# RK4 stage of a conditioned four-layer kernel: linear values written into PSUM by VectorE instead of identity products on TensorE

## What is computed

```
def _derivative(q, p, drive, coupling, bias):
    i_couple = jnp.tanh(q) @ coupling.T
    dq = q - q ** 3 / 3.0 - p + drive + i_couple + bias
    dp = EPSILON * (q + ALPHA - BETA * p)
    return (dq, dp)

def _rk4_step(q, p, drive, coupling, bias):
    dq1, dp1 = _derivative(q, p, drive, coupling, bias)
    dq2, dp2 = _derivative(q + 0.5 * DT * dq1, p + 0.5 * DT * dp1, ...)
    dq3, dp3 = _derivative(q + 0.5 * DT * dq2, p + 0.5 * DT * dp2, ...)
    dq4, dp4 = _derivative(q + DT * dq3, p + DT * dp3, ...)
    q_next = clip(q + DT / 6.0 * (dq1 + 2 * dq2 + 2 * dq3 + dq4))
    p_next = clip(p + DT / 6.0 * (dp1 + 2 * dp2 + 2 * dp3 + dp4))
```

## Time and profile before

| what | us |
|---|---|
| three runs | 912.86, 912.0, 912.5 (median 912.5) |
| the profiled execution's own time | 913.69 |
| its span in the trace | 911.7 |
| RK4 stage, all 32 steps | from about 720 to 908 |
| PE busy | 895.2 |
| DVE busy | 605.3 |
| ACT busy | 411.8 |
| POOL busy | 276.8 |

### The profile page before, as it was taken

One profiled execution on the slowest core, in us unless ns is written; L12 is line 12 of the kernel. 1 busy time (PEld: TensorE's weight loads), 2 busy tenths in 40 slices (PEclk: granted clock), 3 DMA queues, 4 the chain that ended last, 5 costly groups with the idle time before them and its releaser, 6 DMA issues.

```text
span 911.7 us, 18478 instructions
## 1 busy us (share of the span) xinstructions
PE 895.2 (98%) x7182; PEld 766.0 (84%) x7182; DVE 605.3 (66%) x1697; ACT 411.8 (45%) x1144; POOL 276.8 (30%) x359
## 2 busy tenths in 40 slices
PE   7999999999999999999999999999999999999998
PEld 5788888888888888888887778899986699999998
DVE  5544555654565544746477875677777788888887
ACT  2233322333223432224346654555545676666665
POOL 2654500011000300014312424333213455554443
PEclk9999999999999999999999999999999999999999
DMA  7222100000000000110014000000000000000000
GB/s 270 75 77 79 39 1 1 2 1 1 2 1 2 1 1 1 47 47 2 1 38 159 0 1 1 1 1 2 1 1 1 1 2 24 1 25 1 25 1 24
DMA packets 5703, 22.00 MB, mean 24 GB/s; under 512 B 880, under 2 KB 1264, under 8 KB 5232
## 3 DMA queue, kind: packets, MB, share of 16 engines
q1 hardware_dynamic: 5616, 20.82, 6.6%
HBM read 18.72 MB, written 2.10 MB: 23 GB/s over the span
## 4 chain that ended last, share of the span: by engine, by line
PE 90%; DVE 7%; ACT 2%; issue 1%; DVEq 0%
PE ps L366 43%; PE ps L774 8%; PE ps L778 7%; PE ps L457 6%; PE ps L635 6%; PE ps L773 5%; PE ps L625 3%; PE ps L637 3%; PE ps L446 2%; DVE g_lo L1273 1%; PE ps L642 1%; PE ps L378 1%; DVE m_lo L1267 1%; DVE frs L1245 1%; PE ps L373 1%
## 5 line engine op out<-in xcount | busy, mean ns | idle before, releaser
L1190 DVE TENSOR_SCALAR qk<-ps,vec 128x512 f32<-128x512 f32 x64 | 48.0, 749 | 99.0 <-PE ps L366 99.0
L366 PE MATMUL ps<-x_hi,W_hi 128*128 128x512 f32 x256 | 102.1, 399 | 3.2 <-DVE x_lo L1313 2.8
L856 ACT ACTIVATE qk<-ps,vec 128x512 f32<-128x512 f32 x64 | 44.2, 690 | 124.9 <-PE ps L366 124.9
L366 PE MATMUL ps<-x_hi,W_lo 128*128 128x512 f32 x256 | 99.8, 390 | 0.0
L366 PE MATMUL ps<-x_lo,W_hi 128*128 128x512 f32 x256 | 99.8, 390 | 0.0
L774 PE MATMUL ps<-rk_th,cpc 128*128 128x128 f32 x516 | 99.0, 294 | 0.1
L1201 DVE SCALAR_TENSOR_TENSOR o_lo<-ps,vec,o_hi 128x512 fp32r<-128x512 f32 x64 | 47.1, 744 | 72.7 <-ACT o_hi L872 69.1
L872 ACT ACTIVATE o_hi<-ps,vec 128x512 fp32r<-128x512 f32 x64 | 44.1, 688 | 111.9 <-PE ps L457 111.9
L774 PEld LDWEIGHTS ps<-rk_th,cpc 128*128 128x128 f32 x516 | 72.7, 191 | 9.3 <-ACT rk_th L1136 6.2
L635 PE MATMUL ps<-ht,hh 128*128 128x128 f32 x512 | 77.0, 283 | 1.0 <-DVE ht L1525 0.9
L773 PE MATMUL ps<-rk_th,cpc 128*128 128x64 f32 x508 | 77.8, 255 | 0.0
(11 more groups left out here) (281 smaller groups left out, 2134.1 us busy)
## 6 DMA issues: line engine op xcount, KB each, us to landing
stage<-qkv_w SPq DMA_DIRECT2D x6, 768.0 KB, 4.5
stage<-out_w SPq DMA_DIRECT2D x4, 512.0 KB, 3.9
f_raw<-ffn_w SPq DMA_DIRECT2D x2, 1024.0 KB, 4.8
xorig<-xT SPq DMA_DIRECT2D x1, 2048.0 KB, 8.2
x_all<-xT SPq DMA_DIRECT2D x1, 1536.0 KB, 15.2
out<-xtb SPq DMA_DIRECT2D x3, 512.0 KB, 3.1
ada_sb<-ada_w SPq DMA_DIRECT2D x1, 1024.0 KB, 9.6
BD<-qkv_w SPq DMA_DIRECT2D x1, 768.0 KB, 6.1
```

The source lines that it names most:

```text
L366: r = pe.matmul(out_, lhsT, rhs, start=first and i == 0, stop=last and i == n - 1)
L856: act.activation(qk[:, 0, h % 2, :], ps[:, PJ[0], :], ACT.Identity, bias=col("qkv_b", HU * u + h)).then_inc(act_evac, 1)
L1190: dve.tensor_scalar(qk[:, 1, h % 2, :], ps[:, PJ[1], :], col("qkv_b", HEADS + HU * u + h), None, ALU.add).then_inc(dve_evac, 1)
```

## The change

In evaluations 1 to 4 of every step DVE writes `E1`, `Z2`, `Z3`, `Z4` straight to the PSUM columns 0 to 63 of the two banks of that evaluation (`seed`), and the identity products go. The coupling products then all run with `start=False` and add to what stands there. Two exceptions are in the first step: evaluation 1 keeps `first_evaluation`, and evaluation 2 keeps `linear(2, "Z2")`. Columns 64 to 127 of these banks, which the `twice` products also write, are never read. After the coupling products of every evaluation but the very first stand five passes of zeros (`keep_warm(WARM_RK)`). `skip_group_check=True` is an argument for the builder and no instruction.

```
-WARM_GRU, WARM_START = 10, 12
+WARM_GRU, WARM_START, WARM_RK = 10, 12, 5
...
             def chunks_in_turn(t, k):
...
                 coupled(k, 1, 1, False, True).then_inc(rk_pe, 1)
+                keep_warm(WARM_RK)
...
             def chunks_together(t, k):
...
                 coupled(k, 1, 1, False, True).then_inc(rk_pe, 1)
+                keep_warm(WARM_RK)
...
                     pe.wait_ge(rk_dve, RK_START + at(t - 1, RK_DVE, "E1"))
-                    linear(1, "E1")
                     chunks_together(t, 1)
...
                 pe.wait_ge(rk_dve, RK_START + at(t, RK_DVE, "Z2"))
-                linear(2, "Z2")
                 if t == 0:
+                    linear(2, "Z2")
                     keep_warm(WARM_START)
                 chunks_in_turn(t, 2)
                 pe.wait_ge(rk_dve, RK_START + at(t, RK_DVE, "Z3"))
-                linear(3, "Z3")
                 chunks_together(t, 3)
                 pe.wait_ge(rk_dve, RK_START + at(t, RK_DVE, "Z4"))
-                linear(4, "Z4")
                 chunks_in_turn(t, 4)
...
+            def seed(k):
+                lo = RK_BANK[k % 2][0]
+                return ps[:, lo:lo + KC, 0:B]
...
-                inc(STT(r_["Z2"], r_["q"], 1 - A_ * C_, r_["U2"], M, Ad))
+                inc(STT(seed(2) if t else r_["Z2"], r_["q"], 1 - A_ * C_, r_["U2"], M, Ad))
...
-                inc(STT(r_["Z3"], r_["q2"], -A_ * C_, r_["t3"], M, Ad))
+                inc(STT(seed(3), r_["q2"], -A_ * C_, r_["t3"], M, Ad))
...
-                inc(STT(r_["Z4"], r_["q3"], 2 * (1 - A_ * C_), r_["b4"], M, Ad))
+                inc(STT(seed(4), r_["q3"], 2 * (1 - A_ * C_), r_["b4"], M, Ad))
...
-                inc(dve.tensor_tensor(r_["E1"], r_[f"D{(t + 1) % 3}"], r_["P"], Su))
+                inc(dve.tensor_tensor(seed(1), r_[f"D{(t + 1) % 3}"], r_["P"], Su))
```

More of the change, by code:

```diff
@@ L772, in coupled @@
                 if last:
-                    return pe.matmul(ps[:, RK_BANK[k % 2][c], 0:B], w, th, start=first, stop=last)
-                return pe.matmul(ps[:, RK_BANK[k % 2][c], 0:2 * B], w, twice(th), start=first, stop=last)
+                    return pe.matmul(ps[:, RK_BANK[k % 2][c], 0:B], w, th, start=first, stop=last, skip_group_check=True)
+                return pe.matmul(ps[:, RK_BANK[k % 2][c], 0:2 * B], w, twice(th), start=first, stop=last, skip_group_check=True)
             def linear(k, z):
                 for c in range(KC):
-                    pe.matmul(ps[:, RK_BANK[k % 2][c], 0:2 * B], ident[:, :], twice(rk[z][:, c, :]), start=True, stop=False)
+                    pe.matmul(ps[:, RK_BANK[k % 2][c], 0:2 * B], ident[:, :], twice(rk[z][:, c, :]), start=True, stop=False, skip_group_check=True)
             def tanh_done(t, k, half):
@@ L808, in first_evaluation @@
                 for c in range(KC):
-                    pe.matmul(ps[:, RK_BANK[1][c], 0:B], ident[:, :], rk["E1"][:, c, :], start=False, stop=True).then_inc(rk_pe, 1)
+                    pe.matmul(ps[:, RK_BANK[1][c], 0:B], ident[:, :], rk["E1"][:, c, :], start=False, stop=True, skip_group_check=True).then_inc(rk_pe, 1)
             for t in range(T):
```

## The result

The change makes the kernel slower: 917.76 us (median of 5 runs, 916.1 to 918.1) against 912.86 for the kernel before in the same comparison. The ratio is 1.0038, 95% interval 1.0023 to 1.0053; the two medians alone would give 1.0054, since the executions before spread from 912.0 to 916.0, so the ratio (3.5 us) is the figure to go by.

A forecast was written before the change was run, and what follows sets the result against it. The prediction took the ring of DVE, ACT and PE latencies as the bound, PE's throughput just under it. Only the moved wait cost: 63 x 0.065 = 4.1 us on 912.5 gave 916.6 us, range 912.2 to 919.5.

The forecast's parts named there:

- The ring: One RK4 step: DVE, ACT and PE latencies from result to reader close at 5.86 us, without the identity products of L778.
- The identity products: PE, evaluations 1 to 4: removing 1.8 us of PE work a step was forecast to gain zero.
- DVE's writes to PSUM: E1, Z2, Z3, Z4 on DVE: taken as zero, with 0.01 us each way for Z2 and Z4, 0.6 us in all.
- the stretches of 1.32 and 1.12: DVE's own chain from qraw to q2 and from q3 to q4, in us, forecast to stay unchanged.
- Zeros: Five passes on PE after the coupling products: about 0.33 us with the entry, forecast to cost nothing in time.
- the 0.04 that the prediction allowed in evaluation 3: Extra us the entry to the zeros could cost on PE before they delayed evaluation 3's coupling load.
- The clock: Rival: PE rests more and its granted clock falls to half; 919 us for one or two falls, chance 0.05.
- The wait that moves: PE's tanh wait, written second, becomes a separate instruction: 0.065 us in the ring in evaluations 2 and 4, 4.1 us in all.
- The 63 places: Evaluations 2 and 4 of every step except evaluation 2 of the first, each paying 0.065 us: 4.1 us.
- The prediction's 0.08 for the same thing on DVE: DVE's next instruction starts 0.11 us after release by a separate wait against 0.03 with its own: difference 0.08.
- PE as the bound: Rival: q2 and q4 hang on PE, so removing identity products gains 7.1 us; 909.5 us with the waits, chance 0.08.
- The cheap wait of 0.02: Rival: PE's separate tanh wait costs only 0.02 us a place, 1.3 us in all, 913.8 us; chance 0.14.

The follow-up runs named there:

- e1: The changed kernel with PE's two waits written the other way round, tanh first and linear value second: 912.14 us, ratio 0.9993, step 5.859 us.
- e2: The changed kernel without PE's waits for the linear value from step 1 on: 913.31 us, ratio 1.0000, step 5.862 us.
- e4: The changed kernel without the passes of zeros (WARM_RK = 0): 916.32 us, ratio 1.0035, step 5.984 us.
- e3: The kernel before with a redundant wait for the linear value ahead of the tanh wait in evaluations 2 and 4: 916.39 us, ratio 1.0037.
- e6: e2 with DVE's two waits ahead of the first half of q2 swapped, its own w first: 912.38 us, ratio 0.9981, step 5.796 us.
- e5: The kernel before with DVE's two waits ahead of the first half of q2 swapped, its own w first: 912.16 us, ratio 0.9984.
- e8: e6 with DVE's U2 moved ahead of the second half of qraw, where DVE waits for PE: 914.91 us, ratio 1.0022, step 5.943 us.
- e7: e5 with DVE's U2 moved ahead of the second half of qraw, identity products kept: 918.1 us, ratio 1.0050, step 6.021 us.
- e11: e8 with POOL's U3 waiting for the moved U2, no identity products: 916.34 us, ratio 1.0025, step 5.946 us.
- e12: e7 with POOL's U3 waiting for the moved U2, identity products kept: 919.1 us, ratio 1.0050, step 6.021 us.

## Why the prediction was right

Forecast 916.6 us in a range from 912.2 to 919.5; measured 917.76. Point by point:

- **The ring, and what is not in it.** Right. It closed before and closes after, and only the pieces named changed. The identity products, 1.8 us of PE a step, were worth nothing: e1 and e2 without them are at 5.86, as before. The page's 98% and its 7% for L778 did not bear on the end.
- **DVE's writes to PSUM.** Right. The linear values take 285 to 295 ns; the stretches of 1.32 and 1.12 are unchanged.
- **Zeros.** Right as to cost in time: e4 without them has the same step. Five took 0.38 of loads, not 0.33, which is 0.01 past the 0.04 that the prediction allowed in evaluation 3; but in e1, where the tanh sits on the load again, the load of evaluation 3 follows the tanh's end by 0.05, so they held nothing up. The clock did not fall without them either: in e4 it stays at 1.00.
- **The wait that moves.** Right in kind and near in size. Forecast 0.065 us a place; the tanh-to-load distance grew by 0.062, from 0.051 to 0.113. Twice a step that is 0.124, and the step grew by 0.117; DVE's two stretches are 0.003 shorter each (medians 1.322 to 1.319 and 1.124 to 1.121). The 63 places would make 3.9 us by this, against the 4.1 of the prediction, and the times of e1 and the changed kernel against their own "before" differ by 0.45%, which is 4.1 us. e3 shows that nothing else is needed for the loss. The prediction's 0.08 for the same thing on DVE was near too: e6 shows 0.07.
- **The rivals.** PE as the bound would have made e1 and e2 faster than before; they are not. By the Trainium skill (Perfetto Trace Analysis, Identifying the Most-Contended Engine) PE's loads, busy for most of the stage, would be what to relieve; e2 took 22 us of loads out of the 176 us (167.29 to 145.32) and the step moved by 0.005. The cheap wait of 0.02 would have given steps of 5.91. The clock did not fall in the stage.
- **What was off.** The effect by the ratio is 3.5 us, against 4.1 forecast; the time itself came out 1.2 us above the forecast. The median before was 912.86 in this comparison and 912.5 in the runs that I built on, which is 0.4 of it; the rest lies within the spread of single executions, and no run separates it further. PE's idle time ahead of evaluation 2 is 0.49, not the 0.6 that the prediction gave.

## What to carry to other kernels

Follow one turn of the loop from result to reader before believing a busy share: an engine at 98% can be out of the ring, and then taking work from it brings nothing. Where two waits stand ahead of one instruction, write first the one that is met last, or drop the one that the other implies; a separate wait cost time only where it was the last to be met, and there it was 0.06 us each time on PE and 0.07 on DVE. Take a second wait off the path only as far as the next one allows: in e5 PE became the last, and 0.02 of the 0.07 stayed. And before moving a DVE instruction, look at what POOL runs at its new place, not only at whether DVE was idle there.

## What the runs showed of the hardware that I had not expected

- **Which wait becomes an instruction.** On both engines the wait written first stays with the instruction and the one written second becomes one of its own. Released by it, PE's load starts 0.113 us after the producer's end and 0.051 without it (changed kernel and e3 against before and e1); DVE's instruction 0.105 and 0.035 (before against e6).
- **DVE beside POOL.** A DVE product of two SBUF inputs took 584 ns in place of 291 to 294 when it started just after a POOL product of 457 ns, and a clip from SBUF to SBUF 471 to 521 ns in place of 227. Instructions with one input in PSUM showed nothing like it: in the kernel before `Z2` starts 0.29 us before a POOL product ends, and takes its 0.29 (by the 0.15 above, `t3` or `U2` there would take an estimated 0.44); `qraw` b, with 0.26 of one left, takes 0.22.

```profile
779.72 0.46 POOL L1959 TENSOR_TENSOR xtb<-xtb,rk_q 128x128 f32<-128x128 f32 x1 [0.30 <-DVE rk_q L1659]
779.89 0.29 DVE L1666 SCALAR_TENSOR_TENSOR rk_Z<-rk_q,ps 128x128 f32<-128x128 f32 x1
```

The Trainium skill (SBUF — State Buffer, Who interferes with whom) states both cases: a DVE instruction with two SBUF inputs contends with a GpSimd instruction that reads SBUF, and so can a `tensor_scalar` in a two-port mode, and the one that issues second is blocked until the first finishes. The runs agree on who waits: in e8 the POOL product started at 784.98, `U2` at 785.01. No run shows which mode the clip ran in. On the length the measurement decides: `U2` ended 0.15 behind the POOL product and not its full 0.29, so about half of it was not held up. Had I set this rule against e7, e8, e11 and e12 beforehand, a gain would have been forecast for none of them.
- **No clock lost.** In e4 PE's loads are busy for 65% of the stage, and the granted clock stays at 1.00 (2.4 GHz).
